# ScalarE computes silu, a norm of ten operations, and gate projections inside the state update

## The chip, the core and the metric

The kernel is one program on one core of a Trainium2 chip. The metric is the device time of one execution in microseconds (us). Three executions of the kernel before took 7752.31, 7766.66 and 7772.56 us; a fourth was profiled.

## What is computed

`x` is [16, 512, 256] in fp32. Two layers follow each other. Layer 0 is a gated delta-rule recurrence over 512 tokens, with 16 heads of 64x64 state for each of the 16 sequences, beside a small expert layer. Layer 1 is attention with a quantized linear layer. The change lies in the recurrence alone:

```python
xn = _layernorm(x)
q = silu(dwconv4(xn @ Wq.T, qcw, qcb))
k = silu(dwconv4(xn @ Wk.T, kcw, kcb)) * 64 ** -0.5
v = silu(dwconv4(xn @ Wv.T, vcw, vcb))
a = sigmoid(xn @ Wa.T + ba)          # a decay for each row of the state
beta = sigmoid(xn @ Wb.T + bb)
# for every token t, S is [64, 64] of each sequence and head:
err = S @ k[t] - v[t]
S = a[t][..., None] * S - beta[t] * (err[..., None] * k[t])
o[t] = S @ q[t]
```

## The kernel before, in words

**Tiling.** The 512 tokens are cut into 32 chunks of C = 16, and the 16 sequences into two groups of GB = 8, so that P = 8*16 = 128 rows (sequence and token) make a tile. A step is one chunk of one group; there are STEPS = 64, and the two groups alternate. Inside a chunk the recurrence is solved in a form with (sequence, head) on the 128 partitions and 64 state rows along them; the state itself lies in `st` and is updated once a chunk.

**Slots.** Every engine runs the same list of slots s = -2..64 (`slot_loop`; slots 4 to 59 in a hardware loop of two slots a turn, so 56 slots). In slot s an engine works for four steps at once, as far as they exist: the norm of step s+2, the convolution, silu, transposes and products of step s+1, the solve of step s, and the state update that step s-1 needs. The order on each engine is the order of the code in `slot`; the engines meet by semaphores alone.

- **VectorE.** Slot: 18 groups of four convolution taps (L674; `conv`, banks 0 to 5, three groups each), with the small norm instructions (L724 to L731, and L94 to L100 in `rsqrt_ops`) one after each group, and six silu products (L688 into `st`, L693 into `z`) after their groups; the decay product L700 over the whole state; two state adds L710 (banks 0 and 1 of the update); then `solve`: 16 rows of L770, L775, L776, L779, with two more state adds after each of the first three rows, and last L786, the update factors `eb`. L786 ends the slot on VectorE.
- **GpSimd.** Slot of step s: key and query dots times beta (L364, L368), the running product of the gates (L370, fourteen L372, L376, L377, L380), then for r = 0..15 L386 (times a gate row) and either L389 (adds a share that ScalarE made: r = 0, 1, 2 and 11 to 15) or L392 and L395. L364 begins the slot on GpSimd. VectorE's first row (COPY L758) waits for L364, and GpSimd's L392 and L389 wait for VectorE's rows.
- **ScalarE.** `evict` of banks 2 to 5 (halo L518, y L519, four L524, which start the convolution sum in PSUM), each followed by a sigmoid L534 of the bank two before; seeds of the solve's rows L566; the keys' copy L542; the shares L579 for rows 0 to 2; `front2` (four evictions L553 and the DMA of v); `products` (eight L588 and a DMA); `front1` (L600, the copy of xnT L603, two gate sigmoids L608 and a DMA, beta L616, L618 and a DMA); `evict` of banks 0 and 1 of step s+2; shares for rows 11 to 15.
- **TensorE.** Projections of banks 2 to 5 (L485), eight banks of the update (L422, two PSUM banks in turn, each waits for VectorE's add), transposes of z (L432), products (L449), then `front1` of step s+2 (transposes of xn L457, gates L463 and L464, beta L467) and projections of banks 0 and 1.
- **SyncE** issues the loads; among them, twice a slot, the decay factors broadcast to 64 partitions (L301), which L700 needs.

The PSUM banks of the convolution are `p_bank` (banks 0, 1, 4, 5) and half of `rows_bank` (2, 3); `rows_bank` also holds the solve's rows, so banks 2 and 3 are projected only after the solve has ended.

Of the kernel before, what the change touches and what calls it, by code (L numbers as in the profile page):

```python
# [58 lines left out]
RSQRT_OPS = 14  # L59
# [61 lines left out]
def layer0_recurrence(nc, ins, o_dram):  # L121
# [9 lines left out]
    decay_dram = [dram(f"decay_dram{g}", [GB * H, DV]) for g in range(GROUPS)]  # L131
    x = ins["L0_attn_x"]

    with ExitStack() as ctx:
# [26 lines left out]
        sg = sb("sg", [128, 2, 4, P])  # L161
# [79 lines left out]
        def _(sp):  # L241
# [15 lines left out]
            def slot(s, n, g, lo, hi):  # L257
# [58 lines left out]
                if updates(lo, hi):  # L316
# [5 lines left out]
                    sp.dma_start(decay_dram[g], acb[:]).then_inc(dec_wr[g], 16)  # L322
# [78 lines left out]
        def _(pe):  # L401
# [10 lines left out]
            def update(s, n, g):
                pe.wait_ge(f_freed, F_USES * s + F1_USES + 2)
                pe.wait_ge(*dma_of(xd_in, n, g, 0, 16 * GB))
                for u in range(8):
# [37 lines left out]
            def front1(s, n, g):  # L453
                bank = use(s, 0)
# [10 lines left out]
                bank = use(s, 3)  # L465
# [23 lines left out]
            def slot(s, n, g, lo, hi):  # L489
# [3 lines left out]
                if updates(lo - 1, hi - 1):  # L493
                    update(s - 1, n - 1 + g, 1 - g)
# [3 lines left out]
                if valid(lo + 2, hi + 2):  # L498
                    front1(s + 2, n + 1, g)
# [6 lines left out]
        def _(act):  # L506
            act.wait_ge(init_done, 1)

            def filled(s, k):
# [1254 lines left out]
```

## Time and profile before

| | |
|---|---|
| three runs | 7752.31, 7766.66, 7772.56 us |
| profiled execution | 7784.81 us, span 7783.0 us |
| recurrence | to about 4805 us of the span |
| TensorE busy | 5243.2 us, 67% of the span |
| VectorE busy | 6164.3 us, 79% |
| ScalarE busy | 3954.5 us, 51% |
| GpSimd busy | 4572.7 us, 59% |

In the profile PE is TensorE's matmul, PEld its weight load, DVE is VectorE, ACT ScalarE, POOL GpSimd, SP SyncE. L12 is line 12 of the kernel. The busy share of an engine is a mean over the two parts of the program; the recurrence is read in a stretch of its own. A matmul in fp32 is recorded as two instructions or more.

### The profile page before, as it was taken

What the parts mean: (1) busy time and instruction counts of PE and PEld (TensorE: products, weight loads), DVE (VectorE), ACT (ScalarE), POOL (GpSimd) and SP (SyncE); (2) the same over time, 40 slices, a digit from 0 to 9 for tenths busy, and PEclk for the clock granted to TensorE, in tenths of its full rate; (3) what the DMA queues carried; (4) which work ended last, traced back from release to release, by engine and by line L of the source; (5) the groups of instructions that cost most, each with busy time, mean ns of one, the idle gap of its engine ahead of it and who ended that gap; (6) DMA issues with size and microseconds to landing.
All of it is one profiled execution on the core that took longest, in us unless ns stands there. A gap on an engine that the chain in (4) does not pass through costs nothing. (4 is left out here: it accounts for less than half of the span.)

```text
span 7783.0 us, 145670 instructions
## 1 busy us (share of the span) xinstructions
PE 5243.2 (67%) x42311; PEld 3481.9 (45%) x42311; DVE 6164.3 (79%) x16516; ACT 3954.5 (51%) x10307; POOL 4572.7 (59%) x4104
## 2 busy tenths in 40 slices
PE   5666665666656666666656561777877777787777
PEld 3544444544545445445445441333433443334433
DVE  7999999999999999999999985556655655656665
ACT  5555555555555555555555552344444444444444
POOL 4989988889889999899989886111111111111110
PEclk7767767767667667677777665788888888888888
DMA  3545545545555455455555452111111121211111
GB/s 93 132 106 118 132 103 121 120 105 132 113 109 131 110 116 128 101 127 123 113 120 124 106 126 60 42 45 41 43 42 41 41 51 49 50 42 41 44 41 34
DMA packets 1453089, 684.05 MB, mean 88 GB/s; under 512 B 1344563, under 2 KB 1396435, under 8 KB 1446100
## 3 DMA queue, kind: packets, MB, share of 16 engines
q1 hardware_dynamic: 1153492, 516.82, 29.8%
q10 hardware_dynamic: 299008, 159.92, 8.5%
q8 instruction: 303, 4.96, 0.3%
q14 instruction: 286, 2.34, 0.1%
HBM read 423.47 MB, written 253.17 MB: 87 GB/s over the span
## 5 line engine op out<-in xcount | busy, mean ns | idle before, releaser
L422 PE MATMUL d_bank<-xd,kt 32*64 32x128 f32 x7936 | 813.7, 384 | 1021.1 <-DVE st L710 1021.1
L386 POOL TENSOR_TENSOR qp<-qp,ab 128x1024 f32<-128x1024 f32 (+15 forms) x1024 | 1413.2, 1380 | 80.4
L422 PEld LDWEIGHTS d_bank<-xd,kt 32*64 32x64 f32 x7936 | 723.7, 201 | 1096.1 <-DVE st L710 1086.2
L674 DVE SCALAR_TENSOR_TENSOR p_bank<-y,conv_w,p_bank 128x128 f32<-128x128 f32 x3072 | 845.1, 345 | 181.7 <-ACT p_bank L524 152.4
L1126 POOL TENSOR_TENSOR ot<-ot,ln_w 128x1024 f32<-128x1024 f32 x64 | 150.6, 2353 | 1404.7 <-ACT ot L1401 1404.7
L485 PE MATMUL p_bank<-xnT,wqkv 128*128 128x128 f32 x4096 | 653.5, 329 | 385.4 <-DVE st L688 384.8
L1545 DVE TENSOR_REDUCE nmax<-w_bank 128x1 f32<-128x512 f32 x1024 | 638.0, 683 | 328.4 <-PE w_bank L1171 319.6
L485 PEld LDWEIGHTS p_bank<-xnT,wqkv 128*128 128x128 f32 x4096 | 613.7, 239 | 426.4 <-issue 426.4
L395 POOL TENSOR_TENSOR qp<-qp,pt 128x832 f32<-128x832 f32 (+7 forms) x512 | 760.6, 1486 | 40.1
L579 ACT ACTIVATE pt<-vb,qp 128x64 f32<-128x64 f32 x1920 | 472.2, 334 | 504.9 <-DVE vb L770 394.6
L779 DVE TENSOR_TENSOR rows_bank<-rows_bank,t 128x960 f32<-128x960 f32 (+14 forms) x960 | 671.2, 699 | 32.9
L392 POOL TENSOR_TENSOR pt<-qp,vb 128x832 f32<-128x832 f32 (+7 forms) x512 | 685.2, 1338 | 0.0
L775 DVE TENSOR_TENSOR rows_bank<-rows_bank,ab 128x960 f32<-128x960 f32 (+14 forms) x960 | 661.9, 690 | 0.0
L776 DVE TENSOR_TENSOR t<-rows_bank,vb 128x960 f32<-128x960 f32 (+14 forms) x960 | 653.2, 680 | 0.0
L1131 POOL TENSOR_TENSOR x1b<-x,bias 128x256 f32<-128x256 f32 x64 | 46.4, 725 | 1010.0 <-DVE bst L1641 1010.0
L1375 ACT ACTIVATE pt<-e_bank 128x1024 f32<-128x1024 f32 x512 | 508.1, 1019 | 104.7 <-PE e_bank L1201 101.6
L579 ACT ACTIVATE share<-vb,qp 128x64 f32<-128x64 f32 x1920 | 472.9, 340 | 76.4 <-DVE vb L770 76.0
L1171 PE MATMUL w_bank<-ks,qs 96*128 96x512 bf16 x1024 | 402.5, 446 | 75.0 <-DVE nmax L1545 33.4
L463 PE MATMUL f_bank<-wa,xnT 128*128 128x512 f32 x512 | 364.2, 850 | 122.9 <-ACT xnT L603 122.9
L449 PE MATMUL p_bank<-st 64*32 64x80 f32 x16384 | 383.0, 243 | 88.5 <-issue 57.0
L372 POOL TENSOR_TENSOR eb<-eb,ab 128x64 f32<-128x64 f32 x896 | 397.1, 443 | 70.4
L674 DVE SCALAR_TENSOR_TENSOR rows_bank<-y,conv_w,rows_bank 128x128 f32<-128x128 f32 x1536 | 427.2, 345 | 0.0
(209 smaller groups left out, 11510.9 us busy)
## 6 DMA issues: line engine op xcount, KB each, us to landing
decay_or_prod<-decay_dram SPq DMA_DIRECT2D x124, 1024.0 KB, 13.0
prod_dram<-decay_or_prod ACTq DMA_DIRECT2D x64, 1280.0 KB, 10.0
kp<-prod_dram SPq DMA_DIRECT2D x64, 640.0 KB, 7.5
qp<-prod_dram SPq DMA_DIRECT2D x64, 640.0 KB, 5.4
a_dram<-at ACTq DMA_DIRECT2D x64, 512.0 KB
v_dram<-vt ACTq DMA_DIRECT2D x64, 512.0 KB
vb<-v_dram SPq DMA_DIRECT2D x64, 512.0 KB, 5.7
ab<-a_dram SPq DMA_DIRECT2D x64, 512.0 KB, 9.3
```

The source lines that it names most:

```text
L386: link(nc.gpsimd.tensor_tensor(q, q, ab[:, g, r:r + 1, :].to_broadcast([128, w, DV]), ALU.mult), 0 if shared else 1)
L392: link(nc.gpsimd.tensor_tensor(pt2[:, 0:w], qp[:, g, r:C, DV + r:DV + r + 1].to_broadcast([128, w, DV]), vb[:, g, r:r + 1, :].to_broadcast ...
L395: link(nc.gpsimd.tensor_tensor(q, q, pt2[:, 0:w], ALU.add))
L422: mm = nc.tensor.matmul(d_bank[u % 2][64 * par:64 * par + 64, 128 * k:128 * k + 128], kt[32 * q:32 * q + 32, g, DK * h:DK * h + DK], xd[32 ...
L485: mm = nc.tensor.matmul(bank[:, 128 * i:128 * i + 128], wqkv[:, k, 128 * m:128 * m + 128], xnT[:, g, k, :], start=k == 0, stop=k == 1)
L579: last = nc.scalar.activation(shares_of(r)[:, t - r], vb[:, g, r, :], ACT.Copy, scale=qp[:, g, t, DV + r:DV + r + 1])
L674: nc.vector.scalar_tensor_tensor(out=zz, in0=y[:, m, :, tap:tap + C], scalar=conv_w[:, m, tap:tap + 1], in1=zz, op0=ALU.mult, op1=ALU.add) ...
L775: link(nc.vector.tensor_tensor(rows, rows, ab[:, g, r:r + 1, :].to_broadcast([128, w, DV]), ALU.mult), 1)
L776: link(nc.vector.tensor_tensor(t2[:, 0:w], column.to_broadcast([128, w, DV]), vb[:, g, r:r + 1, :].to_broadcast([128, w, DV]), ALU.mult))
L779: link(nc.vector.tensor_tensor(rows, rows, t2[:, 0:w], ALU.add))
L1375: nc.scalar.activation(pt[:, kt % 2, 2 * pr:2 * pr + 2], e_bank[pr][:], ACT.Exp, scale=float(D1) ** -0.5).then_inc(e_freed, 1)
L1545: nc.vector.tensor_reduce(nmax[:, n:n + 1], bank[:], AX.X, ALU.max, negate=True).then_inc(freed, 1)
```

## The change

Four things are changed, all in `layer0_recurrence`.

1. ScalarE writes silu of the convolution bank itself, into `st` or `z`. The tile `sg`, the sigmoid and VectorE's product are gone. The scale of the keys, 1/8, was folded into the convolution's weights; now the copies of the keys (place_keys, front2) apply it.
2. The norm's reciprocal root uses tensor_scalar with two operands each: two instructions for a Newton round in place of four, and mhalf = -(var+eps)/2 ahead. From the first shift's operand on (var) to the last there are ten.
3. `front1` is split. TensorE does transposes and gates between banks 1 and 2 of the state update, beta after bank 7. ScalarE copies xnT between silu 3 and silu 4, does the gates' sigmoids behind the keys' copy and beta behind the first shares. The uses of the `f_bank` buffers are counted in the new order (front1_use, front2_use).
4. The decay factors lie in DRAM as [parity, row] instead of interleaved, so that the broadcast reads one run of 16 KB for each partition; the write does the reordering.

```diff
-    decay_dram = [dram(f"decay_dram{g}", [GB * H, DV]) for g in range(GROUPS)]
+    decay_dram = [dram(f"decay_dram{g}", [2, GB * HP, DV]) for g in range(GROUPS)]
...
-                        rows = decay_dram[o].rearrange("(m two) i -> two m i", two=2)[par:par + 1]
-                        sp.dma_start(db[64 * par:64 * par + 64], rows.to_broadcast([64, GB * HP, DV])).then_inc(db_in[o], 16)
+                        rows = decay_dram[o][par:par + 1].to_broadcast([64, GB * HP, DV])
+                        sp.dma_start(db[64 * par:64 * par + 64], rows).then_inc(db_in[o], 16)
...
-                    sp.dma_start(decay_dram[g], acb[:]).then_inc(dec_wr[g], 16)
+                    sp.dma_start(decay_dram[g].rearrange("two m i -> m two i"), acb[:]).then_inc(dec_wr[g], 16)
...
                 if updates(lo - 1, hi - 1):
-                    update(s - 1, n - 1 + g, 1 - g)
+                    update(s - 1, n - 1 + g, 1 - g, (0, 1))
+                if valid(lo + 2, hi + 2):
+                    gates(s + 2, g)
+                if updates(lo - 1, hi - 1):
+                    update(s - 1, n - 1 + g, 1 - g, (2, 3, 4, 5, 6, 7))
+                if valid(lo + 2, hi + 2):
+                    betas(s + 2, g)
                 if valid(lo + 1, hi + 1):
                     front2(s + 1, n + g, 1 - g)
                     products(s + 1, n + g, 1 - g)
                 if valid(lo + 2, hi + 2):
-                    front1(s + 2, n + 1, g)
                     for j in range(2):
                         project(s + 2, g, j)
...
-                nc.scalar.activation(sg[:, j % 2], conv_bank(j).rearrange("p (m t) -> p m t", m=4), ACT.Sigmoid,
-                                     scale=float(DK) ** 0.5 if j // 2 == 1 else 1.0).then_inc(sg_ready, 1)
+                if j == 0 and due(8 * (s - 1)):
+                    act.wait_ge(p_filled, 8 * (s - 1))
+                if j == 2 and due(s):
+                    act.wait_ge(f_filled, front2_use(s - 1) + F2_USES)
+                bank = conv_bank(j)
+                if j < 2:
+                    nc.scalar.activation(st[g][:, :, 4 * j:4 * j + 4, DV + C:DV + 2 * C],
+                                         bank.rearrange("p (h b t) -> p b h t", h=4, b=GB), ACT.Silu).then_inc(silu_done, 1)
+                else:
+                    nc.scalar.activation(z[:, 4 * j - 8:4 * j - 4, :], bank.rearrange("p (h t) -> p h t", h=4),
+                                         ACT.Silu).then_inc(silu_done, 1)
...
-                rsqrt_ops(nc, rs[:], var[:], rstmp[:], link)
+                link(nc.vector.tensor_scalar(mhalf[:], mv[:, 1:2], EPS, -0.5, ALU.add, ALU.mult))
+                link(nc.vector.tensor_scalar(rstmp[:].bitcast(i32), var[:].bitcast(i32), 1, None, ALU.logical_shift_right))
+                link(nc.vector.tensor_scalar(rs[:].bitcast(i32), rstmp[:].bitcast(i32), -1.0, RSQRT_MAGIC, ALU.mult, ALU.add))
+                for _ in range(RSQRT_STEPS):
+                    link(nc.vector.tensor_scalar(rstmp[:], rs[:], rs[:], mhalf[:], ALU.mult, ALU.mult))
+                    link(nc.vector.tensor_scalar(rs[:], rstmp[:], 1.5, rs[:], ALU.add, ALU.mult))
```

On TensorE, one slot of the loop from the projections of banks 2 and 3 on (xn, wa and wbeta are the norm, the gates' and the betas' operands, xd and kt those of the update, z the silu outputs, st the state), before:

```order
L485 MATMUL rows_bank<-xnT,wqkv 128x128 x16
L485 MATMUL p_bank<-xnT,wqkv 128x128 x16
L422 MATMUL d_bank<-xd,kt 64x128 x64
L432 MATMUL f_bank<-ident,z 128x128 x16
L449 MATMUL p_bank<-st 32x80 x128
L457 MATMUL f_bank<-ident,xn 128x128 x2
L463 MATMUL f_bank<-wa,xnT 128x512 x2
L464 MATMUL f_bank<-ba,ones 128x512
L463 MATMUL f_bank<-wa,xnT 128x512 x2
L464 MATMUL f_bank<-ba,ones 128x512
L467 MATMUL f_bank<-xnT,wbeta 16x128 x2
L485 MATMUL p_bank<-xnT,wqkv 128x128 x16
```

and now:

```order
L501 MATMUL rows_bank<-xnT,wqkv 128x128 x16
L501 MATMUL p_bank<-xnT,wqkv 128x128 x16
L436 MATMUL d_bank<-xd,kt 64x128 x16
L471 MATMUL f_bank<-ident,xn 128x128 x2
L477 MATMUL f_bank<-wa,xnT 128x512 x2
L478 MATMUL f_bank<-ba,ones 128x512
L477 MATMUL f_bank<-wa,xnT 128x512 x2
L478 MATMUL f_bank<-ba,ones 128x512
L436 MATMUL d_bank<-xd,kt 64x128 x48
L483 MATMUL f_bank<-xnT,wbeta 16x128 x2
L446 MATMUL f_bank<-ident,z 128x128 x16
L463 MATMUL p_bank<-st 32x80 x128
```

The seven rows of `front1` have moved from behind the products: transposes and gates into the update, behind two of its eight banks, and beta behind the update.

On ScalarE, the middle of a slot from the sigmoid or silu of bank 3 on (kp are the products' keys, at the gates, kt and vt the transposed z), before:

```order
L534 ACTIVATE sg<-rows_bank 128x512
L534 ACTIVATE sg<-p_bank 128x512
L566 ACTIVATE rows_bank<-kp 128x960
L534 ACTIVATE sg<-p_bank 128x512
L542 ACTIVATE st<-z 128x64x16
L579 ACTIVATE pt<-vb,qp 128x64 x16
L579 ACTIVATE share<-vb,qp 128x64 x15
L579 ACTIVATE pt<-vb,qp 128x64 x14
L553 ACTIVATE kt<-f_bank 128x512 x2
```

and now:

```order
L562 ACTIVATE z<-rows_bank 128x512
L634 ACTIVATE xnT<-f_bank 128x256
L562 ACTIVATE z<-p_bank 128x512
L595 ACTIVATE rows_bank<-kp 128x960
L562 ACTIVATE z<-p_bank 128x512
L570 ACTIVATE st<-z 128x64x16
L641 ACT_TABLE_LOAD
L641 ACTIVATE at<-f_bank 128x512 x2
L645 DMA a_dram<-at 8x16x1024
L608 ACTIVATE pt<-vb,qp 128x64 x16
L608 ACTIVATE share<-vb,qp 128x64 x15
L608 ACTIVATE pt<-vb,qp 128x64 x14
```

The copy of xnT, a table load, two gate sigmoids and a DMA issue now stand ahead of the first shares. The slot's other table load stands ahead of its first silu:

```order
L546 ACTIVATE rows_bank<-rows_bank,conv_b,conv_w 128x128 x4
L559 ACT_TABLE_LOAD
L559 ACTIVATE st<-p_bank 128x8x4x16
L540 ACTIVATE halo<-rows_bank 128x96
```

It lies between the evictions of banks 2 and 3; before, only the sigmoid lay there.

## Rows read from the trace of the kernel before

**Rows 1.** Windows, four slots: sum and mean busy us of each engine.

```profile
sum 298.50, PE 193.90 PEld 150.83 DVE 274.41 ACT 164.37 POOL 256.06; mean PE 48.48 PEld 37.71 DVE 68.60 ACT 41.09 POOL 64.02
```

**Rows 2.** Timeline, GpSimd: start us, us, instruction, count, idle before and releaser.

```profile
387.25 0.69 POOL L364 TENSOR_TENSOR kp<-kp,nb 128x240 f32<-128x240 f32 x1 [0.71 <-POOL qp L389]
...
2083.49 0.69 POOL L364 TENSOR_TENSOR kp<-kp,nb 128x240 f32<-128x240 f32 x1 [0.29 <-POOL qp L389]
...
2085.13 9.77 POOL L372 TENSOR_TENSOR eb<-eb,ab 128x64 f32<-128x64 f32 x14
...
2133.51 2.15 POOL L392 TENSOR_TENSOR pt<-qp,vb 128x576 f32<-128x576 f32 x1
...
2155.14 0.69 POOL L364 TENSOR_TENSOR kp<-kp,nb 128x240 f32<-128x240 f32 x1 [0.87 <-POOL qp L389]
...
2178.45 2.36 POOL L389 TENSOR_TENSOR qp<-qp,pt 128x1024 f32<-128x1024 f32 x1 [11.06 <-ACT pt L579]
...
2232.81 0.69 POOL L364 TENSOR_TENSOR kp<-kp,nb 128x240 f32<-128x240 f32 x1 [0.29 <-POOL qp L389]
...
4505.68 0.69 POOL L364 TENSOR_TENSOR kp<-kp,nb 128x240 f32<-128x240 f32 x1 [0.51 <-POOL qp L389]
```

**Rows 3.** GpSimd's waits, in the loop and in slots 60-62: us, times, longest.

```profile
POOL qp L389 <- ACT pt L579: 168.0, 39, 11.1
...
POOL qp L389 <- ACT pt L579: 25.6, 3, 13.8
```

**Rows 4.** Timeline, VectorE, slots 26 and 27.

```profile
2061.99 1.59 DVE L786 TENSOR_TENSOR eb<-vb,eb 128x1024 f32<-128x1024 f32 x1
...
2071.14 0.68 DVE L688 TENSOR_TENSOR st<-p_bank,sg 128x512 f32<-128x512 f32 x1
2071.74 0.14 DVE L95 TENSOR_SCALAR norm_work<-norm_work 128x1 int32<-128x1 int32 x1
...
2088.71 4.42 DVE L700 TENSOR_TENSOR st<-st,decay_or_prod 128x4096 f32<-128x4096 f32 x1
...
2132.32 2.31 DVE L786 TENSOR_TENSOR eb<-vb,eb 128x1024 f32<-128x1024 f32 x1
2140.51 2.17 DVE L674 SCALAR_TENSOR_TENSOR p_bank<-y,conv_w,p_bank 128x128 f32<-128x128 f32 x8 [5.87 <-ACT p_bank L524]
```

**Rows 5.** GpSimd's line 372: ns min/median/max.

```profile
L372 POOL TENSOR_TENSOR eb<-eb,ab x896: 317/319/4607, 93.7 to 4746.5; 128x64 f32<-128x64 f32 x180
```

**Rows 6.** Timeline, TensorE, the same slots.

```profile
2079.61 1.96 PE L422 MATMUL d_bank<-xd,kt 32*64 32x128 f32 x32
2094.39 3.68 PE L422 MATMUL d_bank<-xd,kt 32*64 32x128 f32 x32 [12.81 <-DVE st L710]
...
2119.91 0.44 PE L457 MATMUL f_bank<-ident,xn 128*128 128x128 f32 x2
2122.34 3.78 PE L463 MATMUL f_bank<-wa,xnT 128*128 128x512 f32 x4 [1.99 <-ACT xnT L603]
...
2133.76 1.04 PE L467 MATMUL f_bank<-xnT,wbeta 128*16 128x128 f32 x4
2134.72 5.23 PE L485 MATMUL p_bank<-xnT,wqkv 128*128 128x128 f32 x32
```

**Rows 7.** VectorE's waits, in the loop and from 4505.7 us on.

```profile
DVE p_bank L674 <- ACT p_bank L524: 91.8, 26, 6.9
...
DVE rows_bank L758 <- POOL kp L364: 20.3, 1, 20.3
```

**Rows 8.** ScalarE: group of the table loads before L600; timeline of slot 27.

```profile
L600 ACT ACT_TABLE_LOAD x1 | 1.3, 1283 | 0.7 <-PEq L1758 0.7
...
2083.42 0.60 ACT L534 ACTIVATE sg<-p_bank 128x512 f32<-128x512 f32 x1 [0.92 <-DVE p_bank L674]
...
2095.30 3.93 ACT L579 ACTIVATE pt<-vb,qp 128x64 f32<-128x64 f32 x16 [6.12 <-DVE vb L770]
```

**Rows 9.** DMA issues: KB each, us to landing.

```profile
decay_or_prod<-decay_dram SPq DMA_DIRECT2D x124, 1024.0 KB, 13.0
```

More of the change, by code:

```diff
@@ L28, with front1_use, front2_use @@
 F_USES = F1_USES + F2_USES
+def front1_use(s):
+    return 0 if isinstance(s, int) and s == 0 else F_USES * s - F2_USES
+def front2_use(s):
+    return F_USES * s + (F2_USES if isinstance(s, int) and s == STEPS - 1 else F_USES)
 F_BANKS = 2
@@ L404, in _, with use, update @@
             pe.wait_ge(init_done, 1)
-            def use(s, k):
-                if due(F_USES * s + k - F_BANKS + 1):
-                    pe.wait_ge(f_freed, F_USES * s + k - F_BANKS + 1)
+            def use(first, k):
+                if due(first + k - F_BANKS + 1):
+                    pe.wait_ge(f_freed, first + k - F_BANKS + 1)
                 return f_bank[k % F_BANKS]
[L412 to L415, printed above, removed]
+            def update(s, n, g, banks):
+                if banks[0] == 0:
+                    pe.wait_ge(f_freed, front2_use(s) + 2)
+                    pe.wait_ge(*dma_of(xd_in, n, g, 0, 16 * GB))
+                for u in banks:
                     q, hh = u // 2, u % 2
@@ L428, in front2 @@
                 for j in range(4):
-                    bank = use(s, F1_USES + j)
+                    bank = use(front2_use(s), j)
                     pe.wait_ge(silu_done, CONV_BANKS * s + j + 3)
@@ L451, in products, with gates @@
                     mm.then_inc(p_filled, 1)
-            def front1(s, n, g):
-                bank = use(s, 0)
+            def gates(s, g):
+                bank = use(front1_use(s), 0)
                 pe.wait_ge(xn_ready, s + 1)
@@ L464, in front1, with betas @@
                     nc.tensor.matmul(bank[:], ones[:], ba[:, 512 * j:512 * j + 512], start=False, stop=True).then_inc(f_filled, 1)
-                bank = use(s, 3)
+            def betas(s, g):
+                bank = use(front1_use(s), 3)
                 for k in range(2):
@@ L601, in front1, with transposed, gates @@
                 act.wait_ge(halo_done, s + 1)
-                bank = filled(s, 0)
+            def transposed(s, g):
+                bank = filled(front1_use(s), 0)
                 nc.scalar.activation(xnT[:, g].rearrange("p k t -> p (k t)"), bank[:, 0:2 * P], ACT.Copy).then_inc(f_freed, 1)
+            def gates(s, n, g):
                 if due(dma_of(a_wr, n, g, -1)[1]):
@@ L612, in front1, with betas @@
                 act.dma_start(a_dram[g].rearrange("t b h i -> b t (h i)"), at[:]).then_inc(a_wr[g], 16)
-                bank = filled(s, 3)
+            def betas(s, n, g):
+                bank = filled(front1_use(s), 3)
                 if due(dma_of(beta_wr, n, g, -1)[1]):
@@ L627, in slot @@
                         evict(s + 1, 1 - g, j)
-                        sigmoid(s + 1, j - 2)
-                    sigmoid(s + 1, CONV_BANKS - 2)
+                        silu(s + 1, 1 - g, j - 2)
+                if valid(lo + 2, hi + 2):
+                    transposed(s + 2, g)
+                if valid(lo + 1, hi + 1):
+                    silu(s + 1, 1 - g, CONV_BANKS - 2)
                 if valid(lo, hi):
@@ L632, in slot @@
                 if valid(lo + 1, hi + 1):
-                    sigmoid(s + 1, CONV_BANKS - 1)
+                    silu(s + 1, 1 - g, CONV_BANKS - 1)
                     place_keys(s + 1, 1 - g)
+                if valid(lo + 2, hi + 2):
+                    gates(s + 2, n + 1, g)
                 if valid(lo, hi):
                     shares(s, g, FIRST_SHARES)
+                if valid(lo + 2, hi + 2):
+                    betas(s + 2, n + 1, g)
                 if valid(lo + 1, hi + 1):
@@ L640, in slot @@
                 if valid(lo + 2, hi + 2):
-                    front1(s + 2, n + 1, g)
+                    left(s + 2, g)
                     for j in range(2):
@@ L713, in norm @@
             def norm(s, n, g, meanwhile):
-                base, made = (3 + RSQRT_OPS) * s, [0]
+                base, made = NORM_OPS * s, [0]
                 def link(ins):
@@ L800, in more_taps @@
                         conv(s + 1, k)
-                        if k % (TAPS - 1) == TAPS - 2 and k >= TAPS - 1:
-                            silu(s + 1, 1 - g, k // (TAPS - 1) - 1)
                 if valid(lo + 2, hi + 2):
```

66 lines of the change are left out of this document (23 added, 43 removed).

## The prediction, made before the change was run

> **What bounds the kernel now.** I read windows of single slots first, then the waits of GpSimd and VectorE, then the timelines of slots 27 and 28, next to each other. Two parts follow each other: the recurrence up to about 4805 us and the rest of the network, which the change leaves alone. All of the argument is about the first.
>
> There VectorE looks like the bound: 68.6 us busy a slot, on average over four slots of together 298.5 us [rows 1], 92%. From the end of one L786 to the next are 71.05 us (2063.58 to 2134.63) [rows 4], under the mean of 74.6: the slots alternate. GpSimd shows why that matters. In the loop, from 387.25 to 4505.68, its 56 slots take 4118.4 us, 73.54 each [rows 2]. Its only long wait is the one of L389 for the first ScalarE share, 168.0 us in 39 slots, 3.0 us a slot [rows 3]. The rest is work and gaps of some 0.1 us between instructions.
>
> So GpSimd has a floor near its present pace. Slot 27 (2083.49 to 2155.14) takes 71.65 us, and no wait for another engine is in it. What is in it: the 14 products L372, whose median is 0.319 us, take 9.77 us [rows 2], because one of them took 4.6 [rows 5], 4.28 us more. It began as VectorE began the decay product L700, 4.42 us at 2088.71 [rows 4]. While that product of two SBUF tensors runs, GpSimd stands. In slot 28 the product came later and fell into GpSimd's wait of 11.06 us, and cost it nothing. Slot 28 took 2232.81-2155.14 = 77.67 us [rows 2]; without its wait and with the 4.28 us that a working GpSimd must then pay, 70.9. A pair of slots has the floor (71.65+70.9)/2 = 71.3 us.
>
> What makes every second slot long is neither engine's work: it is the chain TensorE to ScalarE to VectorE. At 2119.91 TensorE begins the norm's transposes, then gates and betas, and only at 2134.72 projects the next convolution banks [rows 6]; VectorE, done at 2134.63, waits 5.87 us for them [rows 4]. Waits of this kind (L674 for ScalarE's L524) are 91.8 us in the loop [rows 7]. VectorE then comes late with the decay and its first row, ScalarE with the share, and GpSimd waits.
>
> **Silu on ScalarE.** Six products L688 and L693 leave VectorE. Each occupies 0.60 us, from its start to the next (2071.14 to 2071.74) [rows 4]: 3.6 us a slot. ScalarE's sigmoid L534 becomes a silu of the same 512 elements. No row shows a silu; below stands the 0.60 us of the sigmoid [rows 8], above I put 1.2, if the strided write of two banks halved the pace. I take 0.60, the same shape from the same bank; at 1.2 it would be 3.6 us more on an engine that is busy 41 of 74.6 us [rows 1]. Moving the key scale into L542 and L553 adds no instruction.
>
> **Table loads.** The built program has ACT_TABLE_LOAD twice a slot, before the first silu and before the gates' sigmoids; before, there were three in all, of 1283 ns [rows 8]. So ScalarE gains 2.6 us a slot. The second is covered: it stands ahead of the shares, where ScalarE waits 6.12 us [rows 8]. The first comes between banks 2 and 3 of the convolution; it moves silu 0, and with it the projection of bank 4, by up to 1.3 us, which VectorE, now quicker there by three silus, may meet as a wait for the eviction of bank 4 or 5. I count 0 to 1.5 us of new idle on VectorE.
> The Trainium skill (ScalarE: Activation LUTs, What ACT_TABLE_LOAD costs) puts a switch of sets at about 2.66 us with its drain, and the same page's Table sets advises to batch calls by set, which speaks against this change. By that price ScalarE would carry 5.3 us a slot instead of 2.6; the trace has the load at 1283 ns and does not show a drain apart.
>
> **The norm.** Three rounds of L97 to L100 and two integer steps become mhalf, two integer steps and three rounds of two. Five instructions fewer at about 0.07 us of issue are 0.4 us. xn now stands after tap group 13 instead of at the end, on VectorE ahead of nothing that waits.
>
> **Gates inside the update.** This takes transposes and gates (2119.91 to 2133.76, 13.9 us in that slot) out of the chain behind the products [rows 6]. Betas move ahead of the transposes of z. The gates now run where TensorE waited 12.81 us for L710 [rows 6]. The two banks after that idle took 3.68 us, the two ahead of it 1.96 [rows 6]: the low of the two levels (1.2 GHz) behind an idle, the high one ahead of it. The new wait is for xn, then for ScalarE's copy of xnT. Behind it on TensorE stand banks 2 to 7 of the update, and VectorE waits for those. Counted from the end E of L786: update banks 0 and 1 from E+16.0 (2079.61) to E+18; transposes and copy, 2.43 us as in 2119.91 to 2122.34, to E+20.4; two gate banks, 11.4 us at the low level (2122.34 to 2133.76), to E+31.8, or at 1.96/3.68 of it to E+26.5; banks 2 and 3 to E+35.5, or E+28.5. VectorE adds them from about E+31 on. At the low level it stands some 3 us, at the high one not at all. On ScalarE the gates delay the first share: second sigmoid at E+32.4, the issue of its DMA 0.6 us, 3.93 us of shares [rows 8]: E+37. In slot 27 it was ready at 2099.23 = E+35.7, and GpSimd did not wait. That is 1.3 us of wait while VectorE keeps its lag behind GpSimd, and none as soon as it runs ahead.
>
> **The decay broadcast.** Two transfers read rows of 16 KB instead of 256 B. They landed a median 13.0 us after issue [rows 9]; the decay moves up by some 4 us, so that their speed could have begun to matter. I cost it at nothing, bounds -1 and +1 us on VectorE's slot.
>
> **The sum.** VectorE's quick slot: 71.05-3.6-0.4 = 67.0 us, with 0 to 1.5 us of idle in the taps and 0 to 3 us at the update 67 to 71.5, most likely 68. That is below GpSimd's 71.3. So VectorE gains some 3 us a slot on GpSimd, until its first row waits for GpSimd's key dots; the last slot shows such a wait, L758 for L364, 20.3 us [rows 7]. From then on GpSimd never waits, the decay always finds it at work, and the period is 71.3 us. For the loop: 4118.4-56*71.3 = 126 us. The waits say the same: 168.0 less about ten decays of 4.28 us that were hidden in them. Slots 60 to 62, unrolled behind the loop, hold 25.6 us of this wait in three slots [rows 3]; two of the three waits, over 10 us each, hid a decay, so at most 17 us go, and I take 12. Slots 1 to 3 I leave at nothing. Together 138 us.
> The profiled execution took 7784.8 us (span 7783.0), 18 us over the median of 7766.7. 7784.8-138 = 7647 on its scale, 7629 on that of the median.
>
> **Rivals.**
> 1. VectorE stays the bound and all its savings show: 68 us a slot, (73.5-68)*59 = 325 us: 7442. For it speaks its 92%; against it slot 27, in which GpSimd had no wait and no room. It would take a GpSimd that the decay doesn't stop.
> 2. A part of the waits stays, because shares come late at ScalarE or the gates run at the low level. With 72.8 us a slot 41 us are left, 7726; with 72.3, 69 us, 7698.
> 3. Slower, by the gates in the update: the copy of xnT stands on ScalarE behind the eviction of bank 5 and silu 3, and TensorE holds banks 2 to 7 behind it. VectorE's slot grows one for one with the end of the gates. From 70 us (low level, 3 us of stand) it passes the present 73.5 if the gates end over 3.5 us later than counted; if they end 6 us later, the slot is 76: 2.5*59 = 147 us more, 7914. Against it: what stands ahead of the copy is under 3 us of work, and gates right behind other matmuls should find the high level.
> 4. GpSimd's floor holds a second stand: L392 of 576 elements began at 2133.51 inside L786, which ended at 2134.63, and took 2.15 us [rows 2, 4]. If VectorE's lead moves that meeting to where it costs nothing, up to 1 us a slot is gained, 59 us: 7570.
>
> **Chances.** Forecast (GpSimd sets 71.3 us, rival 4 as its lower edge) 0.80; rival 1 0.04; rival 2 0.09, half of it within 0.3% (23 us, about what a measurement of this kernel can tell from no change); rival 3 0.07. Faster by over 0.3%: 0.80+0.04+0.04 = 0.88; within it 0.05; slower 0.07. The range takes in rival 4 and the nearer half of rival 2: 7565 to 7700.
>
> **What would show it.** Right: L389 no longer waits for ScalarE; GpSimd's slots take 71 to 72 us each and don't alternate; VectorE's new long wait is that of its first row (the COPY into rows_bank) for L364, 3 to 5 us a slot; every decay meets a GpSimd instruction longer by 4.28 us; VectorE's waits for the eviction (L546 now) are gone; silu 0.6 us. Wrong: long waits of VectorE for d_bank or of GpSimd for pt, or a period below 70 us.

## The result, and the profile after

Four runs of the changed kernel took 7624.28 to 7628.97 us, median **7626.86**; the kernel before, its three runs and a fourth beside these, has a median of 7767.68. The ratio is 0.9822, 95% interval 0.9805 to 0.9839: 141 us faster. The forecast was 7629, in a range of 7565 to 7700.

Lines that keep their work have new numbers: key dots L364 is now L376, L386/L389/L392/L395 are L398/L401/L404/L407, L786 is L813, the taps L674 are L714, the decay L700 is L722, its broadcast L301 is L313, the state adds L710 are L732, the first row's COPY L758 is L785, the eviction L524 is L546.

GpSimd's timeline of one slot in the middle of the loop (columns as in [rows 2]), with the first row of the loop ahead of it and the first row behind the loop at its end:

```profile
379.95 4.12 POOL L376 TENSOR_TENSOR kp<-kp,nb 128x240 f32<-128x240 f32 x1 [0.71 <-POOL qp L401]
...
2018.73 0.69 POOL L376 TENSOR_TENSOR kp<-kp,nb 128x240 f32<-128x240 f32 x1 [0.29 <-POOL qp L401]
...
2058.60 2.42 POOL L398 TENSOR_TENSOR qp<-qp,ab 128x640 f32<-128x640 f32 x1
...
2083.22 0.45 POOL L398 TENSOR_TENSOR qp<-qp,ab 128x128 f32<-128x128 f32 x1
2083.83 4.47 POOL L401 TENSOR_TENSOR qp<-qp,share 128x128 f32<-128x128 f32 x1 [0.16 <-POOL qp L398]
...
2090.04 0.69 POOL L376 TENSOR_TENSOR kp<-kp,nb 128x240 f32<-128x240 f32 x1 [0.87 <-POOL qp L401]
...
4364.62 0.69 POOL L376 TENSOR_TENSOR kp<-kp,nb 128x240 f32<-128x240 f32 x1 [0.51 <-POOL qp L401]
```

From 379.95 to 4364.62 are 3984.7 us for 56 slots, 71.15 each, where it was 73.54 [rows 2]. The slot shown takes 71.3. Of the 56, 47 take 70.7 to 71.7, where it was 71.5 to 77.7. The other nine lie between 66.7 and 75.6: there the decay falls behind the end of one slot, and a slot behind it holds two. In the slot shown L401 of 128 elements took 4.47 us, where its neighbour L398 of the same 128 elements took 0.45: it began 0.26 us behind VectorE's decay product (2083.57 to 2087.99). The other long one, L398 at 2058.60, began while VectorE's L813 ran (2057.12 to 2059.60).

The waits tell the rest. First GpSimd's, then VectorE's, both between 400 and 4400 us (total us, times, longest us):

```profile
POOL qp L401 <- POOL qp L398: 71.0, 446, 0.2
POOL kp L376 <- POOL qp L401: 32.1, 56, 0.9
...
POOL qp L401 <- ACT share L608: 0.2, 1, 0.2
```

```profile
DVE st L722 <- DMA decay_or_prod<-decay_dram: 136.3, 56, 6.7
DVE rows_bank L785 <- POOL kp L376: 72.9, 51, 2.8
DVE p_bank L714 <- DVE eb L813: 19.8, 24, 0.9
DVE norm_work L746 <- DMA xt<-in_L_attn_x: 5.6, 7, 1.7
DVE p_bank L714 <- ACT p_bank L546: 3.2, 4, 1.1
```

GpSimd's 168.0 us of waits for a share [rows 3] are 0.2. What is left is waits for its own instructions. VectorE, which waited 91.8 us for evictions [rows 7], waits 3.2. In their place stand two waits, in nearly every slot: 136.3 us for the decay broadcast and 72.9 us for GpSimd's key dots. Of the two only the second had been forecast.

Windows of four slots, as [rows 1]:

```profile
sum 285.00, PE 198.68 PEld 152.20 DVE 261.71 ACT 176.06 POOL 263.68; mean PE 49.67 PEld 38.05 DVE 65.43 ACT 44.01 POOL 65.92
```

VectorE went from 68.60 to 65.43 us a slot and GpSimd from 64.02 to 65.92, because every decay now falls into its work. The busiest engine of before is now level with GpSimd.

The spans differ by 7783.0-7622.5 = 160.5 us, the medians by 141. The profiled execution of before lay 17 us over its median, that of after 3 under. Of the 160.5 us, 133.7 are the loop, 23.0 slots 60 to 62 (234.0 and 211.0 us), 4.8 slots 0 to 3, 2.5 what stands ahead of them, and 3.6 were lost behind the last slot.

### The profile page after: what moved, and what is told of

The parts are those of the page before. It is cut to its first block and busy times, and to the rows that moved or that the text cites. A ratio compares the mean times of both kernels' runs of the same rounds, so it can differ in the third digit from the quotient of the medians.

```text
span 7622.5 us, 144906 instructions
## 1 busy us (share of the span) xinstructions
PE 5357.4 (70%) x42311; PEld 3522.9 (46%) x42311; DVE 5931.4 (78%) x15810; ACT 4097.8 (54%) x10434; POOL 4603.9 (60%) x4104
## 5 line engine op out<-in xcount | busy, mean ns | idle before, releaser
L398 POOL TENSOR_TENSOR qp<-qp,ab 128x1024 f32<-128x1024 f32 (+15 forms) x1024 | 1533.7, 1498 | 80.4
L436 PE MATMUL d_bank<-xd,kt 32*64 32x128 f32 x7936 | 776.3, 372 | 408.2 <-DVE st L732 402.7
L436 PEld LDWEIGHTS d_bank<-xd,kt 32*64 32x64 f32 x7936 | 688.4, 192 | 520.6 <-DVE st L732 507.5
L714 DVE SCALAR_TENSOR_TENSOR p_bank<-y,conv_w,p_bank 128x128 f32<-128x128 f32 x3072 | 833.4, 347 | 67.9 <-ACT p_bank L546 42.7
L407 POOL TENSOR_TENSOR qp<-qp,pt 128x832 f32<-128x832 f32 (+7 forms) x512 | 760.3, 1485 | 40.1
L501 PE MATMUL p_bank<-xnT,wqkv 128*128 128x128 f32 x4096 | 607.2, 316 | 219.9 <-ACT st L559 179.7
L501 PEld LDWEIGHTS p_bank<-xnT,wqkv 128*128 128x128 f32 x4096 | 579.5, 229 | 248.4 <-issue 248.2
L404 POOL TENSOR_TENSOR pt<-qp,vb 128x832 f32<-128x832 f32 (+7 forms) x512 | 630.9, 1232 | 0.0
L501 PE MATMUL rows_bank<-xnT,wqkv 128*128 128x128 f32 x2048 | 357.3, 356 | 326.7 <-DVE eb L813 326.7
L608 ACT ACTIVATE share<-vb,qp 128x64 f32<-128x64 f32 x1920 | 473.3, 340 | 72.9 <-DVE vb L797 72.4
L501 PEld LDWEIGHTS rows_bank<-xnT,wqkv 128*128 128x128 f32 x2048 | 347.2, 269 | 336.7 <-issue 336.7
L401 POOL TENSOR_TENSOR qp<-qp,share 128x960 f32<-128x960 f32 (+5 forms) x384 | 462.8, 1205 | 57.0 <-POOL qp L398 53.2
L463 PE MATMUL p_bank<-st 64*32 64x80 f32 x16384 | 400.0, 251 | 119.3 <-issue 96.0
## 6 DMA issues: line engine op xcount, KB each, us to landing
decay_or_prod<-decay_dram SPq DMA_DIRECT2D x124, 1024.0 KB, 13.3
```

The lines of the kernel that those rows point to most:

```text
L398: link(nc.gpsimd.tensor_tensor(q, q, ab[:, g, r:r + 1, :].to_broadcast([128, w, DV]), ALU.mult), 0 if shared else 1)
L404: link(nc.gpsimd.tensor_tensor(pt2[:, 0:w], qp[:, g, r:C, DV + r:DV + r + 1].to_broadcast([128, w, DV]), vb[:, g, r:r + 1, :].to_broadcast ...
L407: link(nc.gpsimd.tensor_tensor(q, q, pt2[:, 0:w], ALU.add))
L436: mm = nc.tensor.matmul(d_bank[u % 2][64 * par:64 * par + 64, 128 * k:128 * k + 128], kt[32 * q:32 * q + 32, g, DK * h:DK * h + DK], xd[32 ...
L501: mm = nc.tensor.matmul(bank[:, 128 * i:128 * i + 128], wqkv[:, k, 128 * m:128 * m + 128], xnT[:, g, k, :], start=k == 0, stop=k == 1)
L608: last = nc.scalar.activation(shares_of(r)[:, t - r], vb[:, g, r, :], ACT.Copy, scale=qp[:, g, t, DV + r:DV + r + 1])
```

## Experiments

Ten kernels were run. Where one needs few words, it stands in the table. The time of a slot is that of GpSimd from slot 4 to 59, read from the first and the last L376 (or its like) as above. "Ratio" is to the kernel before, run beside it.

| kernel | median us | ratio, 95% interval | us a slot |
|---|---|---|---|
| before | 7767.7 to 7782.0 by batch | 1 | 73.54 |
| changed | 7626.9 | 0.9822, 0.9805 to 0.9839 | 71.15 |
| gates_and_norm | 7628.7 | 0.9804, 0.9788 to 0.9821 | 71.07 |
| silu_alone | 7631.1 | 0.9810, 0.9792 to 0.9828 | 71.40 |
| norm_alone | 7719.4 | 0.9913, 0.9879 to 0.9947 | 72.34 |
| taps_halved | 7614.1 | 0.9788, 0.9772 to 0.9805 | 71.08 |
| decay_small | 7375.2 | 0.9478, 0.9457 to 0.9500 | 67.16 |
| pool_longer | 7731.5 | 0.9954, 0.9938 to 0.9970 | 72.97 |
| old_broadcast | 7613.1 | 0.9798, 0.9782 to 0.9814 | 70.89 |
| no_table_switch | 7619.1 | 0.9798, 0.9781 to 0.9814 | 71.10 |
| shared9 | 7509.9 | 0.9664, 0.9648 to 0.9680 | 69.43 |
| shared9_db | 7519.6 | 0.9660, 0.9631 to 0.9689 | 69.57 |

### Which engine sets 71.15 us

**taps_halved** takes work from VectorE; the taps of half of the sequences are left out:

```diff
-                        out=zz, in0=y[:, m, :, tap:tap + C], ..., in1=zz,
+                        out=zz[:, 0:GB // 2], in0=y[:, m, 0:GB // 2, tap:tap + C], ..., in1=zz[:, 0:GB // 2],
```

> The changed kernel; the convolution's 72 tap instructions of a slot work on half of the sequences, the other half's taps are left out, some 4 to 5 us less of VectorE a slot. Theory (GpSimd is the bound): no change, 7615 to 7630 us, and VectorE's waits for the decay's DMA and for L376 grow by the same 4 to 5 us a slot. Rival (VectorE is still the bound, its waits are short enough to be noise): 62 slots times 4 us, 7380 us.

Line 714 of the changed kernel, then of this one (ns min/median/max):

```profile
L714 DVE SCALAR_TENSOR_TENSOR p_bank<-y,conv_w,p_bank x3072: 318/348/364, 35.1 to 4494.9; 128x128 f32<-128x128 f32 x192
```

```profile
L714 DVE SCALAR_TENSOR_TENSOR p_bank<-y,conv_w,p_bank x3072: 254/281/293, 34.9 to 4486.0; 128x64 f32<-128x64 f32 x192
```

72 taps a slot, each 67 ns shorter, are 4.8 us. The slot stayed at 71.08. All of VectorE's waits together rose from 4.3 to 8.5 us a slot, nearly as much as the taps had given; the longest (400 to 4300 us):

```profile
DVE st L722 <- DMA decay_or_prod<-decay_dram: 268.6, 55, 7.2
DVE rows_bank L785 <- POOL kp L376: 75.8, 50, 2.6
DVE rows_bank L714 <- ACT rows_bank L546: 72.8, 70, 1.3
```

So VectorE's work is not the bound. But the wait for the broadcast doubled and the one for key dots did not move, which leaves a second suspect: the broadcast's chain. That is what old_broadcast and shared9_db are for.

**pool_longer** gives GpSimd one more product a slot, just ahead of L388; VectorE waits for none of it directly:

```diff
+        idle = sb("idle", [128, C, DV])
...
+                nc.gpsimd.tensor_tensor(idle[:], ab[:, g, 0:C], ab[:, g, 0:C], ALU.mult)
```

> The changed kernel with one more GpSimd instruction a slot, a product of 128x1024 elements into a tile that nobody reads, 2.4 us as L398 of the same size. Theory (GpSimd never waits): all of it shows, 64 slots times 2.4 to 2.5 us, 7777 us, the time of the kernel before. Rival (VectorE is as much the bound): part of it is hidden, under 7700 us.

```profile
L389 POOL TENSOR_TENSOR idle<-ab x64: 1893/1894/1896, 98.5 to 4696.7; 128x1024 f32<-128x1024 f32 x64
```

The product took 1.89 us, less than the expectation had put on it; with the 0.08 us to the next instruction the slot should grow by some 1.9. It grew from 71.15 to 72.97, by 1.82: nearly one for one. The expected 7777 us rested on a product of 2.4 us; the time was 7731.5.

**decay_small** takes the stand away that the decay product puts on GpSimd (it multiplies 4 of the state's 64 blocks and leaves the rest out):

```diff
-                nc.vector.tensor_tensor(sv..., sv..., db[:], ALU.mult).then_inc(decayed, 1)
+                few = sv.rearrange("p b h i -> p (b h) i")[:, 0:4]
+                nc.vector.tensor_tensor(few, few, db[:, 0:4], ALU.mult).then_inc(decayed, 1)
```

> The changed kernel; the decay product touches 4 of its 64 blocks of state, the rest is left out, so 4.4 us become 0.3. Theory (the product stops GpSimd for its whole length): no GpSimd instruction is longer by 4.28 us any more, its slot falls from 71.1 to 66.9 us, 7370 us. Rival (GpSimd is slow there for a reason of its own): its slot stays at 71 and the time at 7620.

Line 376 of the changed kernel and then of this one, and this one's decay:

```profile
L376 POOL TENSOR_TENSOR kp<-kp,nb x64: 687/688/4542, 86.2 to 4575.6; 128x240 f32<-128x240 f32 x64
```

```profile
L376 POOL TENSOR_TENSOR kp<-kp,nb x64: 687/689/693, 92.2 to 4331.1; 128x240 f32<-128x240 f32 x64
...
L723 DVE TENSOR_TENSOR st<-st,decay_or_prod x62: 424/428/881, 169.6 to 4263.7; 128x256 f32<-128x256 f32 x62
```

The product fell from 4.43 to 0.43 us, by 4.00, and no L376 was stretched to 4.5 us any more. The slot fell from 71.15 to 67.16, by 3.99. VectorE lost the same 4.0 us here, so this run alone would not say through which engine the time went. taps_halved does: 4.8 us of other VectorE work moved nothing. The stand of GpSimd is worth its full length.

### What the parts are worth

**silu_alone** is the kernel before with silu on ScalarE and nothing else; **gates_and_norm** is the kernel before with the gates in the update and the new norm; **norm_alone** has the norm only. The cores of the edits:

```diff
 # silu_alone
-                nc.scalar.activation(sg[:, j % 2], ..., ACT.Sigmoid, ...).then_inc(sg_ready, 1)
+                nc.scalar.activation(st[g]... or z..., bank..., ACT.Silu).then_inc(silu_done, 1)
 # gates_and_norm
-                    update(s - 1, n - 1 + g, 1 - g)
+                    update(s - 1, n - 1 + g, 1 - g, (0, 1))
+                    gates(s + 2, g)
+                    update(s - 1, n - 1 + g, 1 - g, (2, 3, 4, 5, 6, 7))
+                    betas(s + 2, g)
 # gates_and_norm and norm_alone
-                rsqrt_ops(nc, rs[:], var[:], rstmp[:], link)
+                link(nc.vector.tensor_scalar(mhalf[:], mv[:, 1:2], EPS, -0.5, ALU.add, ALU.mult))
...
+                    link(nc.vector.tensor_scalar(rstmp[:], rs[:], rs[:], mhalf[:], ALU.mult, ALU.mult))
+                    link(nc.vector.tensor_scalar(rs[:], rstmp[:], 1.5, rs[:], ALU.add, ALU.mult))
```

> The kernel before with silu on ScalarE alone; norm, place of the gates and broadcast as before. Theory: the chain from the products over transposes, gates and projections to the eviction of bank 0 stays, VectorE only waits longer for it; the slots still alternate and 0 to 40 us are gained: 7730 to 7768 us. Rival (VectorE's own work was the bound): 3.6 us of each of 62 slots, 7540 to 7640 us, or down to GpSimd's floor, 7626.

> The kernel before with the gates inside the update and the norm of ten operations alone; sigmoid and product, and the interleaved broadcast, stay as before. Theory (GpSimd's floor of about 71.2 us a slot; what kept it from it was VectorE's wait for the projections behind the gates): the alternation goes, VectorE's slot is 70.6 us plus 0 to 1.5, so 71.2 to 72 us a slot and 7630 to 7680 us in all. Rival (the gain came from the 3.6 us that VectorE no longer spends on silu products): 7740 to 7768 us, since those products are still there.

> The kernel before with the new norm alone: five instructions fewer on VectorE in a slot, some 0.4 us, and xn after tap group 13; silu, gates and broadcast as before. The silu alone (3.6 us less on VectorE) and the gates with the norm (13.9 us less in the chain) each brought GpSimd to its floor of 71.1 to 71.4 us a slot, about 7630. Theory: it takes some 3 us a slot, on VectorE's work or in its chain, to make GpSimd's waits for the share (3.0 us a slot) go; 0.4 us gives back no more than itself, 0 to 24 us: 7745 to 7770, the slots of GpSimd still alternate and L401 (L389 of before) still waits for ScalarE's share some 150 us in the loop. Rival: the alternation is unstable and any small relief ends it: about 7630, no wait for the share.

Silu alone and gates with norm each bring the whole gain: 71.40 and 71.07 us a slot. That silu alone would, was not expected. VectorE's waits of silu_alone, then those of gates_and_norm, 400 to 4300 us:

```profile
DVE p_bank L707 <- ACT p_bank L542: 106.6, 35, 8.8
...
DVE rows_bank L707 <- ACT rows_bank L542: 30.7, 43, 1.1
```

```profile
DVE p_bank L708 <- ACT p_bank L547: 4.2, 5, 0.8
```

With silu alone the chain TensorE to ScalarE to VectorE is as long as before, and VectorE still waits for it, 106.6+30.7 = 137 us where it was 91.8 in a slightly longer window [rows 7]. But it is busy 66.2 us a slot where it was busy 68.7, and so keeps GpSimd's pace in spite of these waits; its lead covers the single late slots: GpSimd waits for a share in `pt` only three times in this window (its waits in silu_alone, us, times, longest):

```profile
POOL qp L401 <- ACT pt L604: 4.0, 3, 1.3
```

With the gates moved the chain itself is gone (4.2 us of waits for the eviction). The gates without the new norm were not tried: there xn comes behind silu 4 on VectorE, whose sigmoid stands on ScalarE behind the copy of xnT, which needs xn. GpSimd's waits in the kernel before were 3.0 us a slot [rows 3]; either of the two parts makes them go, and the second finds nothing left to take.

The norm alone gave 1.2 us a slot, between what theory and rival had said. In its GpSimd waits (400 to 4300 us) the share is there, in 22 places with at most 4.2 us; the kernel before has 36 in the same window, 160.9 us, up to 11.1:

```profile
POOL qp L402 <- ACT pt L598: 55.2, 22, 4.2
```

Over its whole loop these waits are 60.8 us. The prediction's account holds here too: 56*71.3 us and 60.8 are 4054, and the loop took 4051. It also says why the waits fell by 107 us and the loop by 67 only: nine waits of over 10 us had each hidden a decay in the kernel before, and these nine stands of 4.28 us, 38.5 us, GpSimd now pays.

What the expectation had wrong is the price of the five instructions, 0.4 us a slot. VectorE's waits stayed (170.7 us between 400 and 4300, where they were 169.5), but its work fell by 1.1 us a slot. The loop of the kernel before, then that of norm_alone:

```profile
387.25:4505.68 4118.43, 2587.24 (x28736) 2049.03 (x28736) 3849.34 (x9497) 2336.90 (x6819) 3668.24 (x3360) 0.70 0.54 118
```

```profile
383.78:4435.02 4051.24, 2579.48 (x28736) 2022.86 (x28736) 3787.62 (x9187) 2329.94 (x6819) 3705.78 (x3360) 0.71 0.54 120
```

The third busy time is VectorE's: (3849.34-3787.62)/56 = 1.10 us. The reason is in the kernel before, in the old norm's lines and in one instruction of it with the one on GpSimd beside it:

```profile
L97 DVE TENSOR_TENSOR norm_work<-norm_work x192: 137/239/1876, 16.1 to 4592.0; 128x1 f32<-128x1 f32 x192
...
L99 DVE TENSOR_SCALAR norm_work<-norm_work x192: 133/143/154, 16.5 to 4594.2; 128x1 f32<-128x1 f32 x192
```

```profile
978.26 1.60 DVE L100 TENSOR_TENSOR norm_work<-norm_work 128x1 f32<-128x1 f32 x1
```

```profile
978.06 1.79 POOL L377 TENSOR_TENSOR eb<-eb,nb 128x960 f32<-128x960 f32 x1
```

Three of the four instructions of an old Newton round (L97, L98, L100) are products with both inputs in SBUF. They are of one element a partition and take 0.14 us at the least, but up to 1.9 and 2.0: L100 began inside L377 of GpSimd and ended as that did. L99, which has one input there, never took more than 0.154. The new rounds are made of tensor_scalar alone, with one-column operands beside the one tile, and none of theirs took more than 0.28 us. So the norm did more than save five issues: it took away nine products a slot that could stand for GpSimd.

### Broadcast and table loads

**old_broadcast** is the changed kernel with the decay factors interleaved in DRAM, 256 B a row, as before; **no_table_switch** makes the gates and betas without sigmoid, so that no table is loaded in the loop:

```diff
 # old_broadcast
-                        rows = decay_dram[o][par:par + 1].to_broadcast([64, GB * HP, DV])
+                        rows = decay_dram[o].rearrange("(m two) i -> two m i", two=2)[par:par + 1]
 # no_table_switch
-                    nc.scalar.activation(at[:, 512 * j:512 * j + 512], bank[:], ACT.Sigmoid).then_inc(f_freed, 1)
+                    nc.scalar.activation(at[:, 512 * j:512 * j + 512], bank[:], ACT.Copy, scale=0.01).then_inc(f_freed, 1)
...
-                nc.scalar.activation(bt[:], bank[0:H, 0:P], ACT.Sigmoid, bias=bb[:]).then_inc(f_freed, 1)
+                nc.scalar.activation(bt[:], bank[0:H, 0:P], ACT.Identity, bias=bb[:], scale=0.01).then_inc(f_freed, 1)
```

> The changed kernel with the decay factors in DRAM interleaved as before, so that the broadcast reads pieces of 256 B again. The changed kernel's two transfers land 13.3 us after issue, those before 13.0. Theory (the floor is GpSimd's, VectorE has 1.3 us a slot left behind its wait for this DMA): 7620 to 7640 us, and VectorE waits for it as long as now or 1 us more. Rival (the new layout is needed now that the decay comes 4 us earlier): VectorE's slot passes 71.2 us, 7680 us or more.

> The changed kernel with the gates' and betas' sigmoids replaced by a plain scaled copy (this part of the computation is changed), so that ScalarE keeps one table set through the recurrence. Theory (the loads stand beside GpSimd's bound): 7618 to 7628 us; VectorE waits longer for L376 and less for L546. Rival (a switch costs its 1.28 us or more on the path, twice a slot): 7300 to 7470 us.

The DMA packets of the changed kernel and the landing of its broadcast, from its page (the last number; old_broadcast has 13.0):

```profile
DMA packets 953133, 684.14 MB, mean 90 GB/s; under 512 B 836660, under 2 KB 888532, under 8 KB 938197
...
decay_or_prod<-decay_dram SPq DMA_DIRECT2D x124, 1024.0 KB, 13.3
```

The fourth change does not make the broadcast land sooner: 13.3 us with runs of 16 KB, 13.0 with rows of 256 B. The slot is 71.15 and 70.89, the times 7626.9 and 7613.1. These two were not run side by side, and the intervals of their ratios overlap: the fourth change shows no gain, and a loss of 14 us can't be told from none. What did get shorter is the issue on SyncE, with a median of 3.11 us in old_broadcast and 0.58 in the changed kernel.

The table loads cost nothing that can be measured: 71.10 us a slot without, 71.15 with. ScalarE around the first of them in the changed kernel:

```profile
2063.95 1.48 ACT L546 ACTIVATE rows_bank<-rows_bank,conv_b,conv_w 128x128 f32<-128x128 f32 x4
2065.45 1.28 ACT L559 ACT_TABLE_LOAD   x1
2066.74 0.60 ACT L559 ACTIVATE st<-p_bank 128x512 f32<-128x512 f32 x1
```

The load begins 0.02 us behind the eviction and the silu 0.01 us behind the load: the switch takes 1.3 us in all. The Trainium skill (ScalarE: Activation LUTs, What ACT_TABLE_LOAD costs) gives 2.66 us with a drain; the load's length agrees, the drain does not show here, and the measurement decides. The silu took 0.60 us, like the sigmoid it replaces [rows 8].

### Taking work from GpSimd

**shared9** lets ScalarE make the shares from row 9 on, not from row 11. **shared9_db** issues on SyncE the broadcast ahead of the query load as well:

```diff
-SHARED_FROM = 11
+SHARED_FROM = 9
 # shared9_db, in SyncE's slot
-                if valid(lo, hi):
-                    ...
-                    sp.dma_start(qp[:, g], src[:, 1]).then_inc(qp_in[g], 16)
                 if updates(lo - 1, hi - 1):
                     ...
                         sp.dma_start(db[64 * par:64 * par + 64], rows).then_inc(db_in[o], 16)
+                if valid(lo, hi):
+                    ...
+                    sp.dma_start(qp[:, g], src[:, 1]).then_inc(qp_in[g], 16)
```

> The changed kernel with rows 9 and 10 also shared: ScalarE makes the products of these rows (13 small instructions more a slot, some 3.2 us), GpSimd adds them. GpSimd saves its product and keeps one add in each, about 0.95+1.05 us a slot. Theory: the slot falls until VectorE's own 69.9 us (71.2 less its present wait of 1.3 for L376), so 1.3 us of the 2.0: 7550 us, and VectorE's wait for L376 is gone. Rival (ScalarE's 3.2 us come on the path): 7620 us or more.

> The changed kernel with shares from row 9 (7510 us, 69.43 us a slot, GpSimd without a wait for another engine, VectorE waits 97.3 us for the decay broadcast and 12.4 for L376), and with the decay broadcast issued ahead of the query load on SyncE. Theory: GpSimd sets the pace here too; VectorE's wait for the broadcast falls by half or more and its wait for L376 rises by as much; the time stays within 15 us of 7510, slot 69.2 to 69.7. Rival: VectorE is the bound of this version and the broadcast stands in its chain: up to 97/56 = 1.7 us a slot are gained, 7410 to 7440.

GpSimd's row of 448 elements in the changed kernel, three instructions, and in shared9, two:

```profile
2071.84 1.14 POOL L398 TENSOR_TENSOR qp<-qp,ab 128x448 f32<-128x448 f32 x1
2072.94 0.94 POOL L404 TENSOR_TENSOR pt<-qp,vb 128x448 f32<-128x448 f32 x1
2073.96 1.13 POOL L407 TENSOR_TENSOR qp<-qp,pt 128x448 f32<-128x448 f32 x1
```

```profile
2096.13 1.14 POOL L398 TENSOR_TENSOR qp<-qp,ab 128x448 f32<-128x448 f32 x1
2097.43 1.14 POOL L401 TENSOR_TENSOR qp<-qp,share 128x448 f32<-128x448 f32 x1 [0.16 <-POOL qp L398]
```

L404 goes from two rows, 0.94 and 0.84 us. The slot fell by 1.72 us to 69.43, and the time to **7509.9 us**, the fastest version that computes everything. The expectation had allowed 1.3 us, up to VectorE's own 69.9 us, and so 7550: it had counted VectorE's wait for the broadcast as if it were work. VectorE now waits less for GpSimd and a little for ScalarE (400 to 4300 us):

```profile
DVE st L722 <- DMA decay_or_prod<-decay_dram: 97.3, 53, 3.7
DVE rows_bank L714 <- ACT rows_bank L546: 25.1, 40, 1.8
DVE rows_bank L785 <- POOL kp L376: 12.4, 20, 1.4
```

The same rows of shared9_db:

```profile
DVE rows_bank L785 <- POOL kp L376: 69.3, 43, 2.6
...
DVE st L722 <- DMA decay_or_prod<-decay_dram: 19.8, 20, 2.8
```

The broadcast came earlier, 77.5 us of its wait went, 56.9 of them reappeared as a wait for GpSimd, and the slot did not get shorter (69.57). This settles what taps_halved had left open: the broadcast's chain is not the bound, here or in the changed kernel, whose GpSimd has 1.7 us more to do in a slot. VectorE stands at one place or at the other.

## Why the prediction held, step by step

- **GpSimd's floor of 71.3 us a slot**: right, 71.15; the decay's stand is 4.0 us in the slot shown, where 4.28 had been taken. It held for four sets of edits on the VectorE side between 70.9 and 71.4 (gates_and_norm, silu_alone, taps_halved, old_broadcast). pool_longer and decay_small moved it by nearly the length of what they added or took. This step carries the result. That "every second slot" was long before was too simple: slots 27 and 28 were the extremes, and nine of 56 held a wait of over 10 us. The sum went by all the waits, so this did no harm.
- **The waits for the share go**: right, 168.0 to 0.2 us. The loop gave 133.7 us, where 126 had been summed; the difference is 0.15 us a slot in the floor.
- **Slots 60 to 62**: 23.0 us, where 12 had been taken. The term was too small by half. I had set two hidden decays against the 25.6 us of waits, which leaves 17, and rounded down without a reason. What the traces show: the three slots held one stand before and two after, not three, because VectorE has done its last decay before slot 62 begins. So 25.6 less 4.1, and 1.6 us less of another wait of GpSimd behind the loop (6.7 and 5.1): 23.1.
- **Slots 0 to 3 and the start**: 4.8 and 2.5 us, where nothing had been put.
- **The scale**: these misses add up to some 22 us against the spans (160.5 and 138). The median moved by 141 only, because the profiled execution of before lay 17 us over its median and that of after 3 under. That 7629 and 7626.9 lie 2 us apart is luck to this extent: on the scale of the profiled executions 7647 had been written, and 7624 came.
- **VectorE's quick slot**: its sum was right. Between 400 and 4400 us its waits listed above add up to some 240 us, 4.3 a slot; 71.15-4.3 is 66.9, and the working had 67.0. That is in part luck. The norm was costed at 0.4 us and gave 1.1 (norm_alone), 4.7 together with silu's 3.6. VectorE's busy time in the loop fell from 68.7 to 65.4 us a slot, by 3.4: 1.3 us came back, much of it at the update factors, where L786 had a median of 1.60 us and L813 has 2.48. The working had neither. Where VectorE stands was wrong. I expected 3 to 5 us a slot at the first row, for key dots. It stands 2.4 us there ahead of the decay, for the broadcast, and 1.3 us at the first row. The step that failed is that the broadcast was costed at nothing with a bound of 1 us: it was looked at for its speed, not for when it is issued.

VectorE's timeline of the changed kernel around L813 and the decay, with SyncE's issues between them:

```profile
2057.12 2.48 DVE L813 TENSOR_TENSOR eb<-vb,eb 128x1024 f32<-128x1024 f32 x1
...
2077.04 4.22 DVE L714 SCALAR_TENSOR_TENSOR p_bank<-y,conv_w,p_bank 128x128 f32<-128x128 f32 x16
2083.57 4.42 DVE L722 TENSOR_TENSOR st<-st,decay_or_prod 128x4096 f32<-128x4096 f32 x1 [2.31 <-DMA decay_or_prod<-decay_dram]
```

```profile
2059.85 0.35 SPq L283 DMA_DIRECT2D upd_dram<-eb  x1
...
2064.34 4.20 SPq L300 DMA_DIRECT2D xd<-upd_dram  x8
...
2069.14 1.13 SPq L313 DMA_DIRECT2D decay_or_prod<-decay_dram  x2
```

L813 ends at 2059.60. SyncE then writes `eb`, waits for it to land, issues eight loads of xd, the query load and, 9.5 us behind L813, the broadcast, which lands 14.4 us later. VectorE is ready for the decay at 2081.26, 21.7 us behind L813. Before, it was ready after 25.1 us, and the same chain was hidden. The quicker VectorE ran into it. Since GpSimd set the pace, that cost nothing.
- **Gates in the update**: right, they cost nothing. TensorE's rows of a slot at the low level, in which L813 ended at 1988.85:

```profile
2005.62 0.69 PE L471 MATMUL f_bank<-ident,xn 128*128 128x128 f32 x2 [1.92 <-DVE xn L758]
2006.86 3.78 PE L477 MATMUL f_bank<-wa,xnT 128*128 128x512 f32 x4 [0.55 <-ACT xnT L634]
...
2016.29 2.07 PE L478 MATMUL f_bank<-ba,ones 1*128 1x512 f32 x2
```

The transposes begin at E+16.8 and the gates end at E+29.5, where E+18 and E+31.8 had been written for the low level; the granted clock over the gates is 0.50 here. In the loop's 56 slots the gates took from 6.0 us (granted clock 1.00, two slots) to 11.5 (0.50, seven slots), and ended at E+24.5 to E+30.3. So the high level that rival 3 expected behind other matmuls was mostly not there throughout; TensorE had waited 1.92 and 0.55 us just ahead of the gates shown. VectorE lost nothing: its decay began at E+24.0 (2012.84), the two state adds and the first row come behind it, and no wait of L732 for d_bank is among the waits above. Rival 3 needed gates over 3.5 us later than counted.
- **Rival 4**: it did not come. L813 still meets a GpSimd instruction (L398 of 640 elements took 2.42 us, that of 704 beside it 1.69), and takes 2.48 us itself.
- **The parts**: the prediction added silu, norm and gates on VectorE's slot and never asked how much each is needed. The runs show that silu is enough, and that gates with the norm are. Rival 1's 7442 needed GpSimd without its stand; decay_small, where the stand is gone and VectorE has 4 us less as well, came to 7375.

## What to carry to other kernels

Look for the engine whose slot is free of waits for others in the best slots, sum what it does there, stands by a neighbour's instruction included, and take that as the floor: all savings on other engines end at it, and two remedies for one stall don't add. When the bound engine changes, the next gain is on the new one (here one constant that moves two products from GpSimd to ScalarE gave 117 us more), not in more of the same. Price a small instruction by the mean of its records and not by its shortest: five of them were worth 1.1 us a slot here, not 0.4. For a step that moves up in time, follow also the DMA it needs back to its issue, with all that stands ahead of it on that queue.

## What the runs showed of the hardware

- While VectorE works on a product of two SBUF tensors, a GpSimd instruction on SBUF stands for nearly all of its length: 4.43 us of product made 0.45 us of L401 into 4.47, and taking 4.00 us from the product took 3.99 from the slot. It works the other way too: L813 took 2.48 us in most slots, 1.48 in its shortest, and L100, one element a partition, took 1.60 us where it began inside a GpSimd instruction and 0.14 at the least. That is the rule of the Trainium skill (SBUF — State Buffer, Who interferes with whom) on instructions with two SBUF inputs, and the trace agrees.
- A broadcast of 1 MB to 64 partitions twice landed no sooner when its source runs were 16 KB instead of 256 B (13.3 and 13.0 us), with the packets of the whole kernel down from 1453089 to 953133.
- Silu from PSUM into a strided SBUF tile took 0.60 us for 512 elements, as a sigmoid did, and a table switch 1.3 us.
